# Chunk 2's head products behind the last quarter of gate h, and one shared layer-norm root for the last two chunks

## The reference

```python
for _ in range(5):
    a = concat([Af @ (state @ in_W.T + in_b), Af.T @ (state @ out_W.T + out_b), state])
    r = sigmoid(a @ r_W.T + r_b)
    z = sigmoid(a @ z_W.T + z_b)
    h = tanh(concat([a_in, a_out, r * state]) @ h_W.T + h_b)
    state = (1 - z) * state + z * h
out = tanh(state @ o1_W.T + o1_b) @ o2_W.T + o2_b
return layernorm(x + out)        # over the 256 features of a row, eps 1e-5
```

## Time and profile before

| | |
|---|---|
| median of three runs | 981.84 us (979.69, 981.84, 983.99) |
| the profiled execution | 983.18 us, span 981.4 us |
| PE busy | 961.5 us, 98% of the span |
| DVE busy | 765.5 us, 78% |
| ACT busy | 469.7 us, 48% |
| POOL busy | 41.8 us, 4% |

### The profile page before, as it was taken

One profiled execution on the slowest core, in us unless ns is written; L12 is line 12 of the kernel. 1 busy time (PEld: TensorE's weight loads), 2 busy tenths in 40 slices (PEclk: granted clock), 3 DMA queues, 4 the chain that ended last, 5 costly groups with the idle time before them and its releaser, 6 DMA issues.

```text
span 981.4 us, 12040 instructions
## 1 busy us (share of the span) xinstructions
PE 961.5 (98%) x4507; PEld 443.3 (45%) x4507; DVE 765.5 (78%) x1202; ACT 469.7 (48%) x663; POOL 41.8 (4%) x57
## 2 busy tenths in 40 slices
PE   7999999999999999999999999999999999999996
PEld 3444444444444444444444444444444444455445
DVE  4989989888888688867867876787677787745756
ACT  4657566554345346433634553364335435422444
POOL 0310100000000000000000000000000000031101
PEclk9999999999999999999999999999999999999998
DMA  9999995234730455194025607701571482042101
GB/s 335 364 410 362 378 347 150 59 81 103 209 85 1 120 156 101 38 208 131 0 77 153 146 1 166 189 22 33 155 167 22 102 215 65 16 135 86 44 1 44
DMA packets 199787, 134.36 MB, mean 137 GB/s; under 512 B 62257, under 2 KB 191921, under 8 KB 195761
## 3 DMA queue, kind: packets, MB, share of 16 engines
q1 hardware_dynamic: 197424, 125.20, 44.8%
q0 software_dynamic: 2304, 8.39, 2.2%
HBM read 102.11 MB, written 16.78 MB: 121 GB/s over the span
## 4 chain that ended last, share of the span: by engine, by line
PE 79%; DMA 9%; ACT 5%; DVE 4%; issue 2%; SPq 1%; ACTq 0%; DVEq 0%
PE bank L1960 36%; PE bank L2101 19%; PE bank L2079 11%; PE bank L2093 6%; DMA tmp<-in_adj_t 5%; DMA tmp<-in_adj 4%; PE bank L2109 3%; ACT areg L616 3%; PE bank L2174 1%; PE bank L2196 1%; PE bank L2158 1%; PE bank L1885 1%; SPq L413 0%; ACT pq_words L631 0%; ACT areg L811 0%
## 5 line engine op out<-in xcount | busy, mean ns | idle before, releaser
L1960 PE MATMUL bank<-areg,xop_words 128*128 128x512 fp8e4 x1792 | 389.5, 379 | 0.8 <-DVE pq_words L1496 0.8
L1960 PEld LDWEIGHTS bank<-areg,xop_words 128*128 128x128 f16 x1792 | 174.9, 98 | 213.0 <-DVE pq_words L1496 2.7
L811 ACT ACTIVATE areg<-pq_words 128x512 f16<-128x512 f32 x90 | 56.3, 629 | 163.5 <-DVE pq_words L1496 62.5
L2101 PE MATMUL bank<-areg,pq_words 128*128 128x512 f16 x504 | 122.7, 379 | 0.3 <-DVE pq_words L1607 0.3
L1885 PE MATMUL bank<-areg,xop_words 128*128 128x512 fp8e4 x512 | 112.1, 379 | 4.1 <-ACT areg L616 2.1
L2101 PE MATMUL bank<-areg,w 128*128 128x512 f16 x378 | 90.7, 379 | 0.0
L1532 DVE SCALAR_TENSOR_TENSOR areg<-pq_words,areg 128x512 f16<-128x512 f32 x90 | 62.2, 691 | 32.4 <-ACT areg L811 30.6
L1885 PEld LDWEIGHTS bank<-areg,xop_words 128*128 128x128 f16 x512 | 49.7, 98 | 65.5 <-issue 4.2
L616 ACT ACTIVATE areg<-tmp 128x2048 fp8e4<-128x2048 int32 x31 | 59.2, 1915 | 38.2 <-DMA tmp<-in_adj_t 21.4
L2101 PEld LDWEIGHTS bank<-areg,pq_words 128*128 128x128 f16 x504 | 49.2, 98 | 60.1 <-issue 0.8
L2079 PE MATMUL bank<-pq_words,w 128*128 128x512 f16 x288 | 65.4, 379 | 0.0
(11 more groups left out here) (247 smaller groups left out, 1260.1 us busy)
## 6 DMA issues: line engine op xcount, KB each, us to landing
areg<-kept_operands SPq DMA_DIRECT2D x112, 512.0 KB, 4.3
tmp<-in_adj_t SPq DMA_DIRECT2D x16, 1024.0 KB, 8.2
tmp<-in_adj SPq DMA_DIRECT2D x15, 1024.0 KB, 7.7
kept_operands<-xop_words POOLq DMA_DIRECT2D x11, 512.0 KB, 8.1
kept_operands<-areg SPq DMA_DIRECT2D x4, 1024.0 KB, 10.2
areg<-in_x SPq DMA_DIRECT2D x7, 512.0 KB, 4.8
kept_operands<-tmp POOLq DMA_DIRECT2D x5, 512.0 KB, 3.2
pq_words<-in_gate_w SPq DMA_DIRECT2D x6, 384.0 KB, 5.7
```

The lines of the kernel that those rows point to most:

```text
L811: nc.scalar.activation(y_dst(t, g, name)[:, 0, :], src, ACT.Copy, scale=PSC).then_inc(s_yh, 1)
L1960: last = nc.tensor.matmul(dst[:, :], xop[:, m // 2, operand_block(xo, part, m % 2), :], place8[:, mo, m, :], start=first and m == pairs[0] ...
L2101: last = nc.tensor.matmul(dst[:, :], weights(d, wp), yop[:, d, Y_PLACE[name], xp, :], start=False, stop=final and gate < 2 and d == 1 and ...
```

## The change

Three things are done. On TensorE `head_out(2)` moves from behind gate tile 3 to behind the last quarter; for that, the banks of the last hidden and head products are renumbered and a wait moves from the second `last_out` to the first. On DVE chunk 2's residual rows, statistics and aggregates move from ahead of the quarters' updates to behind them, between the last splits. And chunk 2's own root (seed on DVE, Newton steps on POOL) is removed: the variance, the square root on ACT and the finishing steps on DVE now run once, on 128x8, for chunks 2 and 3 together, behind chunk 3's statistics. ACT then normalises row tiles 0, 1 and 2 of chunk 2, and DVE row tile 3 of chunk 2 and all four of chunk 3; the stores wait accordingly.

```diff
         def last_hidden_bank(h, m):
-            return bank[((4, 7), (2, 3))[h][m]]
+            return bank[((4, 7), (0, 1))[h][m]]

         def head_rows(c, j):
             if c == CH - 1:
-                return bank[(0, 1, 5, 6)[j]][:, 0:D]
+                return bank[4 + j][:, 0:D]
@@ SP, store_rows
-                if c < 2 or (c == CH - 1 and h == 0):
-                    sp.wait_ge(s_norm, JC * min(c, 2) + 2 * h + 2)
+                if c < 2:
+                    sp.wait_ge(s_norm, JC * c + 2 * h + 2)
+                elif c == CH - 1:
+                    sp.wait_ge(s_norm, 2 * JC + 1 + 2 * h + 2)
                 else:
-                    sp.wait_ge(s_norm_a, 2 * h + 2 if c == 2 else JC + 2)
+                    sp.wait_ge(s_norm_a, 2 + h)
+                    if h == 1:
+                        sp.wait_ge(s_norm, 2 * JC + 1)
@@ POOL
-            var, a, b, r, mr = [ln_t[:, i, 0:JC] for i in range(5)]
-            pool.wait_ge(s_var, 1)
-            for i in range(NEWTON):
...
@@ ACT, behind last_hidden(3)
+            act.wait_ge(s_var, 1)
+            nc.scalar.activation(ln_t[:, 5, :], ln_t[:, 0, :], ACT.Sqrt).then_inc(s_root, 1)
             act.wait_ge(s_rstd, 1)
-            for j in range(JC):
+            for j in range(JC - 1):
                 normalize_act(CH - 2, j)
-            act.wait_ge(s_var, 2)
-            nc.scalar.activation(ln_t[:, 5, JC:], ln_t[:, 0, JC:], ACT.Sqrt).then_inc(s_root, 1)
-            act.wait_ge(s_rstd, 2)
-            for j in range(JC // 2, JC):
-                normalize_act(CH - 1, j)
@@ DVE
             def last_updates():
+                for i in range(3):
+                    last_update(i)
+                    last_split_lo(i)
+                last_update(3)
                 add_rows(2, range(JC // 2))
+                last_split_lo(3)
+                add_rows(2, range(JC // 2, JC))
                 statistics(2, 0)
                 statistics(2, 1)
-                add_rows(2, range(JC // 2, JC))
+                last_hidden_lo(0)
                 statistics(2, 2)
                 stats = statistics(2, 3)
-                last_update(0)
+                last_hidden_lo(1)
                 ln_link(stats)
                 aggregate(range(JC))
-                last_split_lo(0)
-                first_root()
-                last_update(1)
...
+                last_hidden_lo(2)
+                last_hidden_lo(3)
@@ DVE, the end
             aggregate(range(JC, 2 * JC))
-            variance(1)
-            inverse_root_by_act(1)
-            normalize(CH - 1, JC, range(JC // 2))
+            variance()
+            inverse_root_by_act()
+            normalize(CH - 2, 0, (JC - 1,))
+            normalize(CH - 1, JC, range(JC))
@@ PE
             def last_out(h):
-                if h == 1:
+                if h == 0:
                     pe.wait_ge(s_qact, len(QUARTERS))
...
-                    if t == LAST and c == CH - 1 and gi == 3:
-                        head_out(2)
...
             for i in range(len(QUARTERS)):
                 last_gate(i)
+            head_out(2)
             for h in range(2):
                 last_hidden(h)
```

More of the change, by code:

```diff
@@ L244, in gnn_program @@
         s_qgate, s_qact, s_qzh, s_qnew = sem("s_qgate"), sem("s_qact"), sem("s_qzh"), sem("s_qnew")
-        s_qhh, s_pool = sem("s_qhh"), sem("s_pool")
+        s_qhh = sem("s_qhh")
         s_xr = [sem("s_xr0"), sem("s_xr1")]
@@ L766, in normalize_act @@
             def normalize_act(c, j):
-                at = j if c == CH - 2 else JC + j
-                nc.scalar.activation(y[:, c % 2, j, :], y[:, c % 2, j, :], ACT.Identity, scale=ln_t[:, 3, at:at + 1],
-                                     bias=ln_t[:, 4, at:at + 1]).then_inc(s_norm_a, 1)
+                nc.scalar.activation(y[:, c % 2, j, :], y[:, c % 2, j, :], ACT.Identity, scale=ln_t[:, 3, j:j + 1],
+                                     bias=ln_t[:, 4, j:j + 1]).then_inc(s_norm_a, 1)
             def head_act(c):
@@ L1445, in inverse_root, with variance, inverse_root_by_act @@
                     ln_link(nc.vector.scalar_tensor_tensor(r, b, 1.5, r, ALU.add, ALU.mult))
[L1448 to L1456, removed]
+            def variance():
+                nc.vector.tensor_scalar(ln_t[:, 0, :], ln_mv[:, :, 1], LN_EPS, None, ALU.add).then_inc(s_var, 1)
+            def inverse_root_by_act():
+                var, a, b, r, mr, root = [ln_t[:, i, :] for i in range(6)]
+                dve.wait_ge(s_var, 1)
+                dve.wait_ge(s_root, 1)
                 ln_link(nc.vector.reciprocal(r, root))
@@ L1460, in inverse_root_by_act @@
                 ln_link(nc.vector.scalar_tensor_tensor(r, b, 1.5, r, ALU.add, ALU.mult))
-                nc.vector.scalar_tensor_tensor(mr, ln_mv[:, js, 0], -1.0, r, ALU.mult, ALU.mult).then_inc(s_rstd, 1)
+                nc.vector.scalar_tensor_tensor(mr, ln_mv[:, :, 0], -1.0, r, ALU.mult, ALU.mult).then_inc(s_rstd, 1)
             def normalize(c, at, js):
```

## The result

The changed kernel takes 984.88 us (median of six, 983.23 to 985.62) against 981.80 for the kernel before (six, 979.69 to 983.99): 1.0034, 95% interval 1.0022 to 1.0046. That is slower by 0.34%, within the 0.5% that count as no change. A later comparison on another chip gave 1.0030, 1.0018 to 1.0041. The later times are medians of all executions, the ratios leave out two that stand far above the rest (1271.77 us with the rows in the hole, 5867.77 us without chunk 2's stores).

What follows compares the result with a forecast made beforehand. The prediction took TensorE to bound most of the span, with the chain ending in ACT's normalisation; 1.33 + 0.02 + 0.49 + 1.52 = +3.36 us on the 981.84 median gave 985.2 us, range 982.2 to 988.0.

Steps and rivals of the forecast that it cites:

- 1, 2: TensorE's order and the quarter pipeline: quarters start 2.62 us earlier, last_hidden(0) starts as before, nothing gained at the end: 0.
- step 3: VectorE's last_split_lo(3) still waits for ACT's split, queued behind last_hidden(0); VectorE idles nearly 3 us: 0.
- step 4: Chunk 2's row sums, statistics and aggregates now stand between VectorE's last splits, delaying last_out's last group: +1.33 us.
- 5: One last root over eight columns instead of four, same instructions, table load still hidden: +0.02 us.
- 6: First store on SyncE is now chunk 2's first half, waiting for ACT's second normalisation: +0.49 us.
- Step 7: Four stores instead of two behind the last root, all 1 MB leaving after it: +1.52 us.
- recorded signs of being wrong: Listed: last_split_lo(3) at 966, clock 0.5 during last_out, stores with holes or under 0.76 each, last_hidden(0) not at 966.46.
- Rival A: last_split_lo(3) on VectorE is released once its state is ready, so the quarters' gain gets through: +1.4, 983.3 us; chance 0.06.
- Rival B: TensorE's clock falls during its waits in last_out: +1.2 to +1.85 on the sum, up to 987.0 us; chance 0.05.
- Rival C: Code loading or overlap in the 950 us ahead of the tail moves, either sign: 976 to 990 us; chance 0.12.

Runs made afterwards that it cites:

- the rows in the hole: Changed kernel with chunk 2's row sums 2 and 3, statistics and aggregates ahead of last_split_lo(3) on VectorE: tail 17.33 us; 984.39 us, ratio 1.0047.
- the swap: Changed kernel with last_split_hi(3) ahead of last_hidden(0) in ACT's order: tail 16.25 us; 983.08 us, ratio 1.0025.
- a sister kernel: Changed kernel without the two stores of chunk 2, those output rows not written: tail 17.87 us; 988.00 us, ratio 1.0056.
- the filled holes: Changed kernel with 19 extra unread matmuls in TensorE's two holes, ahead of last_hidden(1)'s second half and last_out(0): tail 18.16 us; 985.00 us, ratio 1.0036.
- the shared root alone: Kernel before with only the root over eight columns, its normalisations and four stores behind it, TensorE and VectorE orders kept: tail 16.97 us; 984.19 us, ratio 1.0037.

## Why the prediction was right

The forecast was 985.2 us and +3.36 in the tail; measured are 984.88 and +3.18. By its own steps:

| step | forecast | measured in the tail |
|---|---|---|
| 1, 2: quarters 2.62 earlier, `last_hidden` unmoved | 0 | 2.62 earlier, 0 |
| 3: `last_split_lo(3)` stays at t+2.63 behind a hole of nearly 3 | 0 | t+2.63, hole 2.78 |
| 4: chunk 2's rows between the splits | +1.33 | +1.16 (last row sums t+7.94 for t+6.78) |
| 5: root over eight columns | +0.02 | +0.05 (root to normalisation, t+12.13 for t+10.92, less step 4) |
| 6: first store later | +0.49 | +0.49 (13.25 - 12.13 for 11.55 - 10.92) |
| 7: two more stores | +1.52 | +1.48 (4.87 us from first issue to end for 3.39) |
| sum | +3.36 | +3.18 |

Two steps are shown by an edit of their own, not only by the difference of two traces. The hold on the wait (step 3) is ACT's order: the swap released it. The shared root with its stores (steps 5 to 7) is 2.03 us alone, against 2.02 in the sum of these rows. Of step 4 the edit into the hole recovered 0.79 of 1.16 us, and the 0.28 us by which the split came late accounts for most of what was left.

Step 4 was 0.17 too high. I spaced each `last_hidden_lo` by 0.38 and the split by 0.45; the trace has 0.32 between a `last_hidden_lo` and what follows it (967.76 to 968.08, 968.75 to 969.07) and 0.40 behind the split, so the third is at t+6.20 for a forecast of t+6.34.

Two of the recorded signs of being wrong are met if their times are taken as they stand: `last_split_lo(3)` starts at 965.91, "at 966" (A), and `last_hidden(0)` at 963.28, not 966.46 (C). The first says nothing for A, since the split still stands 2.63 us behind the first matmul of `last_hidden`; A means t-0.2, which the swap has. The signs should have been given as distances. The second can't decide on C either, since kernels with the order of before start their own tail anywhere from 963.41 to 966.46.

Rival A (the wait doesn't block) was wrong for the changed kernel, and its size is now measured: its swap gave 16.25, +1.3 over the kernel before, for +1.4 forecast. Rival B, the clock, was real and I argued against it with too little. From one execution I read that 2 us of near idleness at 18 us left the clock at 1.00. In four other traces (the changed kernel's second and fifth, the swap's, the rows in the hole) the clock did fall between 19 and 22 us, for some 3.4 us, after a wait of TensorE's at the same place. The second's windows:

```profile
19.00:20.00 1.00, 0.28 (x2) 0.19 (x3) 0.96 (x3) 1.00 (x3) 0.00 (x0) 0.98 0.96 401
20.00:21.00 1.00, 1.00 (x4) 0.35 (x3) 0.96 (x3) 0.34 (x2) 0.00 (x0) 0.50 1.06 442
```

And it fell inside `last_out` in one trace of six with these two holes, at a price of 1.43 us, inside the 1.2 to 1.85 that I had worked out. The Trainium skill (TensorE: Matmul & The Clock Gate, What's actually happening) has the throttled state as the default that activity releases; these traces agree as far as they go: the clock fell behind waits, and without chunk 2's stores it was back at 977.4, while TensorE was at work in `last_out`. What stays open is how often it strikes the changed kernel: five of five traces at full clock and one of a sister kernel don't give a rate, and the filled holes couldn't settle it.

Step 7's sentence on a page can be closed too: by the Trainium skill (DMA: Bandwidth & Descriptors, Anatomy of one DMA), whose figures are for DMAs that GpSimd issues, two more stores would be an estimated 1.20. The trace has 1.48 for these, issued by SyncE, and the forecast's 1.52 from the kernel's own row was the better price.

Rival C, something ahead of the tail, is not excluded. For the changed kernel little is left for it: its time is 3.3 us longer in the first comparison and 2.9 in the second, for 3.18 in the tail. But in the comparison of the four edits (the swap, the rows in the hole, the shared root alone, no stores of chunk 2) the times stand 1.1 to 2.6 us further above the kernel before than the tails do, for the shared root alone 3.6 us for 2.03. All four are compared with the same 16 executions of the kernel before, whose median is 980.26, lower than in the other comparisons (981.1 to 981.8). That sample or the kernels may be the reason; no run tells.

What lies ahead of the tail is in any case most of the scatter: the tail begins at 966.46, 966.03, 963.41 and 964.20 in four traces with the order of before, and at 963.28, 965.81, 964.61, 963.60 and 965.45 in five of the changed kernel. Nearly all of it arises in the first 130 us, where TensorE waits for adjacency rows (the changed kernel's first profile: 1.8 us; its second: 2.9, and a fall of the clock); of the 830 us from 130 to 960 it is busy for 827.4 to 828.1 in every trace. That my median was only 0.3 us off is thus partly luck; the tail, 0.18 off, is the fair test.

## What to carry to other kernels

Before moving work forward on one engine, find its last consumer and read every in-order queue on the way there: here 2.62 us on TensorE ended in front of one instruction that ACT had queued behind an unrelated one, and swapping two lines of ACT was worth more (1.87 us) than the whole reordering lost (1.15). The swapped order without the shared root was not run; by these tails it would stand near 16.25 - 2.03 = 14.2 us, 0.7 below the kernel before, which is an estimate and leaves open where chunk 2's own root would find its place. A transfer that lies under compute is free only while it lies there: merging two roots removed small steps that the chain of waits before doesn't show, and put 0.5 MB of stores behind the last one, 1.5 us. Where a kernel's times scatter by 0.3%, measure edits of 0.1% from an event near the edit to the end, over several traces.

## What the runs showed of the hardware

- The changed kernel's tail repeats within 0.1 us (18.12 to 18.20 in five executions) while its start moves by 2.5 us for the same kernel.
- The granted clock fell between 2.1 and 5.4 us after the last matmul in five executions of the changed kernel, and in one of six traces with the same two holes of about 1 us it fell 0.6 us behind the second; 15 matmuls of the last groups then took 3.35 us on the chain of waits, for 1.92 in the changed kernel's first profile.
- Four 256 KB stores behind each other ran at 321 to 326 GB/s, the DMA engines busy for a share of 0.96 to 0.97; with four of 128 KB it was 0.82, since SyncE issued one in 0.47 us and the engines moved one in 0.39.
- On 128x8 the small VectorE steps took 0.17 us, on 128x4 0.16; the reciprocal 0.20 for 0.18.
